# A graph network's batch-norm stage: the matrix engine's order within a tick, three turned buffers, merged row statistics, and eight tiles kept in SBUF

## The reference

```
x = _layernorm(x + _L2_gnn_ref(x, ...))       # third layer
x = _layernorm(x + _L3_gnn_ref(x, ...))       # fourth layer

# third layer, its end: batch norm over all rows, column by column
mean = jnp.mean(agg, axis=0); var = jnp.var(agg, axis=0)
y = (agg - mean) * jax.lax.rsqrt(var + BN_EPS) * gamma + beta
return jax.nn.relu(y)
# fourth layer, its start
h = (x @ W).reshape(n, heads, ch)             # 256 x 256, and the attention logits
```

## Time and profile before

| what | value |
|---|---|
| median of 3 runs | 6393.06 us (6388.5 to 6402.69) |
| the profiled execution's own time | 6399.0 us |
| its span, first to last instruction | 6397.3 us |
| mean granted TensorE clock over the span | 0.838 of full speed |
| phase n4 in the span, between the barriers | 4319.75 to about 4966.6 us |
| ticks 11 to 101 of n4 | 4367.76 to 4921.69 us |

### The profile page before, as it was taken

How to read it: one execution, slowest core, us unless ns; L and a number is a source line. 1 busy time by engine, 2 the same in 40 slices (tenths; PEclk the granted TensorE clock), 3 DMA queues, 4 the chain that set the end, 5 groups by cost and what they waited for, 6 DMA issues and landing times. The chain is left out here.

```text
span 6397.3 us, 74087 instructions
## 1 busy us (share of the span) xinstructions
PE 4260.0 (67%) x18797; PEld 3091.6 (48%) x18797; DVE 4604.8 (72%) x15011; ACT 3125.1 (49%) x6788; POOL 3809.3 (60%) x3139
## 2 busy tenths in 40 slices
PE   2488882058885988588866678997898477880000
PEld 1177772047774877477512224556777355560000
DVE  5645554644444876699599996968887899957776
ACT  0033331023332665588555556766776377772333
POOL 5767775767774777565255525721111688747776
PEclk9599996579997999799877778998999688895555
DMA  8944446954443997899698888989997678756665
GB/s 315 371 78 79 79 74 193 378 159 80 80 80 78 321 311 280 270 316 316 213 305 295 304 266 327 399 306 324 341 347 287 225 278 292 274 199 233 237 239 196
DMA packets 616389, 1558.26 MB, mean 244 GB/s; under 512 B 126988, under 2 KB 283090, under 8 KB 599038
## 3 DMA queue, kind: packets, MB, share of 16 engines
q1 hardware_dynamic: 430270, 1159.75, 51.8%
q0 software_dynamic: 185696, 393.77, 22.3%
HBM read 794.19 MB, written 811.66 MB: 251 GB/s over the span
## 5 line engine op out<-in xcount | busy, mean ns | idle before, releaser
L864 POOL DMA_INDIRECT NS<-e_tot,e_idx x392 | 633.5, 1616 | 241.5 <-ACT e_tot L1118 92.5
L1802 POOL DMA_INDIRECT l_eg<-HBT,k_nsrc x392 | 481.4, 1228 | 351.9 <-POOLq L161 120.6
L989 DVE TENSOR_SCALAR e_eq<-e_pk,z_skey 128x128 f32<-128x128 f32 x588 | 186.9, 345 | 627.6 <-DMA NS<-e_tot,e_idx 598.1
L2408 PE MATMUL l_pm<-k_w_L3b,l_zt 128*128 128x258 f32 x1568 | 414.2, 424 | 118.5 <-ACT l_o L2467 117.8
L1255 POOL DMA_INDIRECT XH<-n_o,z_home x392 | 384.2, 980 | 165.6 <-issue 113.1
L2382 PE MATMUL l_ps<-l_a,k_ident 128*128 128x512 f32 x392 | 309.0, 881 | 222.9 <-DVE l_a L2660 211.6
L2546 ACT ACTIVATE l_a<-l_a,l_eshare 128x64 f32<-128x64 f32 (+1 forms) x980 | 280.5, 373 | 308.8 <-DVE l_eshare L2064 308.8
L2408 PE MATMUL l_pm<-k_w_L1b,l_zt 128*128 128x264 f32 x1568 | 384.0, 400 | 51.1 <-ACT l_o L2467 50.8
L2022 DVE SCALAR_TENSOR_TENSOR l_erun<-l_erun,k_same,l_eg 128x260 f32<-128x260 f32 (+2 forms) x880 | 414.9, 471 | 3.3 <-issue 0.2
L2408 PEld LDWEIGHTS l_pm<-k_w_L3b,l_zt 128*128 128x128 f32 x1568 | 328.5, 215 | 180.6 <-issue 126.9
L2737 DVE BATCH_NORM_STATS2 l_bs<-l_a 128x6 f32<-128x256 f32 x1016 | 402.1, 413 | 1.3
(11 more groups left out here) (442 smaller groups left out, 13304.1 us busy)
## 6 DMA issues: line engine op xcount, KB each, us to landing
HBT<-l_o SPq DMA_DIRECT2D x196, 528.0 KB, 4.3
l_a<-HBT SPq DMA_DIRECT2D x156, 528.0 KB, 6.0
GSUMS<-l_erun SPq DMA_DIRECT2D x72, 1056.0 KB, 5.9
NS<-z_zero SPq DMA_DIRECT2D x100, 520.0 KB, 9.1
l_a<-XH SPq DMA_DIRECT2D x98, 528.0 KB, 6.0
HA<-n_o SPq DMA_DIRECT2D x98, 528.0 KB, 4.6
l_a<-HA SPq DMA_DIRECT2D x98, 528.0 KB, 6.8
X<-l_z SPq DMA_DIRECT2D x98, 520.0 KB, 7.7
```

The lines of the kernel that those rows point to most:

```text
L864: pool.indirect_dma_start(out=nodes, out_offset=bass.IndirectOffsetOnAxis(ap=idx[q % DEEP][:, k:k + 1], axis=0), in_=tot[q % 2][:, k, :], ...
L1802: pool.indirect_dma_start(out=self.g[b % self.ng][:, k, :], out_offset=None, in_=self.table, in_offset=bass.IndirectOffsetOnAxis(ap=self.i ...
L2408: last = pe.matmul(self.pm[h][:, i, 0:self.wc], zt[:, k, h * (J // 2) + i, :], self.weight[:, k, 0:self.wc], start=k == 0, stop=k == KC - 1)
```

## The change

The change has five parts.

- On PE the order within a tick becomes PROD, TURN, BACK. The lags of all stages stay as they are.
- The buffer `zt` exists three times (RT = 3) and no longer twice, and ACT's wait for it is relaxed to fit.
- `variance` no longer issues eight `bn_aggr` for a pair of tiles but three small operations on all eight rows at once (difference of the two half means, sums, square) and a last one that joins them. The adding of EPS moves from DVE to POOL, as an operation of its own ahead of the power. `shifts` halves the sum of means.
- The last eight tiles before the final one of l3 (KEPT) stay in SBUF: their X2 rows and their sums. l3 doesn't store their sums to AGG, and n4 takes these tiles first (`order`) and doesn't load them. The sums' buffers (RY) become eight and no longer four.
- The loads' waits and the places of the logits follow the new order of tiles.

The diff, cut:

```diff
--- before.py
+++ after.py
 MOVED = 40
+KEPT = [(1, t) for t in range(TR - LATE, TR)]
+KEEP_ROWS = len(KEPT) + 1
...
     LD, YR, BACK, ADD, VAR, NORM, TURN, ZT, PROD, EVICT, STORE = 0, 2, 3, 4, 5, 7, 8, 9, 10, 11, 12
-    RA, RY, RZ, RO = 9, 4, 4, 3
+    RT = 3
+    RA, RY, RZ, RO = KEEP_ROWS, len(KEPT), 4, 3
+    order = KEPT + [(r, t) for r in range(2) for t in range(TR) if (r, t) not in KEPT]
...
-                    if t is not None:
+                    if t is not None and t >= len(KEPT):
+                        n = order[t][0] * TR + order[t][1]
                         if t >= RA:
                             sp.wait_ge(s_z, t - RA + 1)
-                        if t >= RY:
-                            sp.wait_ge(s_y, t - RY + 1)
+                        sp.wait_ge(s_y, t - RY + 1)
                         sp.dma_start(a[t % RA][:], rows(T["X2"], t)).then_inc(s_in[t % RA], 16)
-                        sp.dma_start(y[t % RY][:], agg[:, :, t * BLK:(t + 1) * BLK]).then_inc(s_yin[t % RY], 16)
+                        sp.dma_start(y[t % RY][:], agg[:, :, n * BLK:(n + 1) * BLK]).then_inc(s_yin[t % RY], 16)
...
+                        pool.tensor_scalar(ve[b][:], ve[b][:], EPS, None, ALU.add).then_inc(s_eps, 1)
+                        pool.wait_ge(s_eps, q + 1)
                         pool.tensor_tensor(rs[b][:], ve[b][:], S["minus_half"][:, 0:w], ALU.pow).then_inc(s_rs, 1)
...
                 for tick in range(ticks):
-                    t = tile(tick, BACK)
+                    t = tile(tick, PROD)
                     if t is not None:
-                        pe.wait_ge(s_y, t + 1)
-                        if t >= 1:
-                            pe.wait_ge(s_u, t)
-                        for j in range(J):
-                            for k in range(KC):
-                                last = pe.transpose(py[:, j, k, :], yr[t % 2][:, k, j, :], S["ident"][:])
-                        last.then_inc(s_back, 1)
+                        pe.wait_ge(s_zt, t + 1)
+                        for h in range(2):
+                            if t >= 1:
+                                pe.wait_ge(s_o, 2 * t - 1 + h)
+                            for i in range(J // 2):
+                                for k in range(KC):
+                                    last = pe.matmul(pm[h][:, i, 0:RW], zt[t % RT][:, k, h * (J // 2) + i, :], weight[:, k, :],
+                                                     start=k == 0, stop=k == KC - 1)
+                            last.then_inc(s_m, 1)
                     t = tile(tick, TURN)
                     if t is not None:
                         pe.wait_ge(s_z, t + 1)
...
                             for j in range(J):
                                 last = pe.transpose(pt[:, k, j, :], z[t % RZ][:, j, k * P:(k + 1) * P], S["ident"][:])
                         last.then_inc(s_t, 1)
-                    t = tile(tick, PROD)
+                    t = tile(tick, BACK)
                     if t is not None:
-                        pe.wait_ge(s_zt, t + 1)
-                        for h in range(2):
-                            if t >= 1:
-                                pe.wait_ge(s_o, 2 * t - 1 + h)
-                            for i in range(J // 2):
-                                for k in range(KC):
-                                    last = pe.matmul(pm[h][:, i, 0:RW], zt[t % 2][:, k, h * (J // 2) + i, :], weight[:, k, :],
-                                                     start=k == 0, stop=k == KC - 1)
-                            last.then_inc(s_m, 1)
+                        pe.wait_ge(s_y, t + 1)
+                        if t >= 1:
+                            pe.wait_ge(s_u, t)
+                        for j in range(J):
+                            for k in range(KC):
+                                last = pe.transpose(py[:, j, k, :], yr[t % 2][:, k, j, :], S["ident"][:])
+                        last.then_inc(s_back, 1)
 
...
-                            act.wait_ge(s_m, 2 * (t - 1))
-                        act.activation(zt[t % 2][:], pt[:], ACT.Copy).then_inc(s_zt, 1)
+                        if t >= RT:
+                            act.wait_ge(s_m, 2 * (t - RT + 1))
+                        act.activation(zt[t % RT][:], pt[:], ACT.Copy).then_inc(s_zt, 1)
                     t = tile(tick, NORM)
...
-                        if t < TR:
-                            dve.tensor_copy(S["asd"][:, J * t + j0:J * t + j0 + J // 2, :], pm[h][:, :, D:RW])
+                        if not order[t][0]:
+                            col = J * order[t][1] + j0
...
-                    for j in range(w):
-                        var_lk.link(dve.bn_aggr(mv[b][:, j, :], bs[b][:, j, :]))
-                        if j % 2:
-                            yield
+                    if q >= 2:
+                        dve.wait_ge(s_nb, q - 1)
+                    var_lk.link(dve.tensor_tensor(gap[b][:], bs[b][:, :, 1], bs[b][:, :, 4], ALU.subtract))
+                    yield
+                    var_lk.link(dve.tensor_tensor(mv[b][:], bs[b][:, :, 1:3], bs[b][:, :, 4:6], ALU.add))
+                    yield
+                    var_lk.settle(dve)
+                    var_lk.link(dve.scalar_tensor_tensor(gap[b][:], gap[b][:], 0.25, gap[b][:], ALU.mult, ALU.mult))
+                    yield
                     var_lk.settle(dve)
                     if q >= 2:
                         dve.wait_ge(s_rs, q - 1)
-                    dve.tensor_scalar(ve[b][:], mv[b][:, :, 1], EPS, None, ALU.add).then_inc(s_var, 1)
+                    dve.scalar_tensor_tensor(ve[b][:], mv[b][:, :, 1], 1.0 / D, gap[b][:], ALU.mult, ALU.add).then_inc(s_var, 1)
...
-                    dve.scalar_tensor_tensor(nb[b][:], mv[b][:, :, 0], -1.0, rs[b][:], ALU.mult, ALU.mult).then_inc(s_nb, 1)
+                    dve.scalar_tensor_tensor(nb[b][:], mv[b][:, :, 0], -0.5, rs[b][:], ALU.mult, ALU.mult).then_inc(s_nb, 1)
...
+    def rows_of(self, u):
+        k = self.kept_at.get(self.tiles[u])
+        return self.a[u % self.ra] if k is None else self.kept[0][k]
+
+    def out_of(self, u):
+        k = self.kept_at.get(self.tiles[u])
+        return self.o[u % self.ro] if k is None else self.kept[1][k]
+
...
+        if now and self.kind != "l3b" and now[1:] not in self.kept_at:
             u, region, t = now
...
-            layer_phase(nc, S, "l3", dict(kind="gcn", rows=T["X2"], rw=SW, weight=S["w_L2"], out=T["AGG"], slots=FIRST),
+            kept = ([y.sb(f"rows{b}", [P, J, SW]) for b in range(KEEP_ROWS)], [y.sb(f"sums{b}", [P, KC, J * P]) for b in range(len(KEPT))])
+            layer_phase(nc, S, "l3", dict(kind="gcn", rows=T["X2"], rw=SW, weight=S["w_L2"], out=T["AGG"], slots=FIRST, kept=kept),
                         dict(table=T["X2"], tw=SW, index=S["nsrc32"], acc=T["SUMS"][0:PC, :]), first=12)
-            batch_norm_phase(nc, S, T)
+            batch_norm_phase(nc, S, T, kept)
```

More of the change, by code:

```diff
@@ L1387, in _, with batch_norm_phase @@
                     take_turns(parts)
-def batch_norm_phase(nc, S, T):
+def batch_norm_phase(nc, S, T, kept):
     tag = "n4"
@@ L1394, in batch_norm_phase @@
     LD, YR, BACK, ADD, VAR, NORM, TURN, ZT, PROD, EVICT, STORE = 0, 2, 3, 4, 5, 7, 8, 9, 10, 11, 12
-    RA, RY, RZ, RO = 9, 4, 4, 3
+    RT = 3
+    RA, RY, RZ, RO = KEEP_ROWS, len(KEPT), 4, 3
+    order = KEPT + [(r, t) for r in range(2) for t in range(TR) if (r, t) not in KEPT]
     with Scope(nc, tag) as s:
-        a = [s.sb(f"a{b}", [P, J, SW]) for b in range(RA)]
-        y = [s.sb(f"y{b}", [P, KC, J * P]) for b in range(RY)]
+        a, y = kept
         yr = [s.sb(f"yr{b}", [P, KC, J, P]) for b in range(2)]
@@ L1404, in batch_norm_phase @@
         mv = [s.sb(f"mv{b}", [P, 2 * J, 2]) for b in range(2)]
+        gap = [s.sb(f"gap{b}", [P, 2 * J]) for b in range(2)]
         ve = [s.sb(f"ve{b}", [P, 2 * J]) for b in range(2)]
@@ L1407, in batch_norm_phase @@
         nb = [s.sb(f"nb{b}", [P, 2 * J]) for b in range(2)]
-        zt = [s.sb(f"zt{b}", [P, KC, J, P]) for b in range(2)]
+        zt = [s.sb(f"zt{b}", [P, KC, J, P]) for b in range(RT)]
         py = s.ps("py", [P, J, KC, P])
@@ L1430, in batch_norm_phase @@
         s_frs = s.sem("batch_rstd")
+        s_eps = s.sem("variance_guarded")
         s_bn = s.sem("batch_factors")
@@ L1459, in pair @@
             return (t // 2, J * 2) if 0 <= t < TN and t % 2 else None
-        rows = lambda table, t: tile_rows(table, t // TR, t % TR)
+        rows = lambda table, t: tile_rows(table, *order[t])
         ticks = TN + STORE + 1
@@ L1556, in _ @@
                         act.wait_ge(s_t, t + 1)
-                        if t >= 2:
-                            act.wait_ge(s_m, 2 * (t - 1))
-                        act.activation(zt[t % 2][:], pt[:], ACT.Copy).then_inc(s_zt, 1)
+                        if t >= RT:
+                            act.wait_ge(s_m, 2 * (t - RT + 1))
+                        act.activation(zt[t % RT][:], pt[:], ACT.Copy).then_inc(s_zt, 1)
```

(32 more changed lines are left out.)

## The result

The changed kernel takes 6777.1 us (median of 4 runs, 6769.1 to 6784.9) against 6391.2 (4 runs, 6388.5 to 6402.7) before. The ratio is 1.060, 95% interval 1.0581 to 1.0619: 386 us slower. The forecast was 6815, with a range of 6630 to 6890.

The account below looks back on a forecast made before the run. The prediction took DVE, with POOL's round trip, to set the pace, and a closed chain plus clock loss to replace it: 423.5 - 3 - 1 + 3 = +422 us on 6393.1 makes 6815 us, range 6630 to 6890.

Parts of the forecast that it names:

- What bounded the kernel: Ticks 11 to 101 of n4: DVE sets the pace, POOL's round trip in its path, 6.15 us a tick.
- The closed chain: n4's ticks: eviction, PROD, TURN, BACK, add, eviction close once per tick, 8.96 us at full clock, +252.5 us over 90.
- The hole: PE idle in every tick of n4 from the end of BACK to PROD, 3.33 us.
- The clock: PE's products behind each hole slow down, 1.9 us a tick, making 10.86 us a tick and +423.5 us over 90.
- band of ticks: The main forecast's tick in n4, 10.2 to 11.9 us, chance 0.76, with its own range of 6750 to 6890 us.
- Three turned buffers: ACT's copy into `zt`: worth nothing in the steady ticks; after tick 101 -4 us, or -2 with a slower clock.
- Merged statistics: DVE and POOL in n4: worth 0 in the new chain, between -0.5 and +0.4 us a pair on the old path.
- Kept tiles, tick 10: 24 transfers spared, -1 us at l3's end; the first product group ahead of BACK in tick 10, +3 us.
- The clock holds: Rival for n4: the hole costs no clock, the tick is 8.96 us and the time 6644 us; chance 0.10.
- Losses pile up: Rival for n4: bursts run mostly at 1.2 GHz, tick 12 to 14 us, 6964 us at 12.5; chance 0.06.
- Not slower: Rival for n4: PROD needn't wait for its own tick's eviction, DVE keeps the pace, about 6387 us; chance 0.08.

Follow-up runs that it names:

- e5: The changed kernel, PE's new order kept, with DVE's whole eviction put ahead of shifts and the add: 6321.2 us, ratio 0.9881.
- e8: The changed kernel with PE's old order (BACK, TURN, PROD) and DVE's shifts moved behind the add: 6320.1 us, ratio 0.9887.
- e1: The changed kernel with PE's order alone put back to BACK, TURN, PROD: 6380.8 us, ratio 0.9973.
- e3: The changed kernel with 22 transpositions of the identity on PE ahead of each PROD, filling its hole: 6641.4 us, ratio 1.0389.
- e4: The changed kernel, PE's new order kept, with DVE's whole eviction put behind shifts but ahead of the add: 6392.4 us, ratio 0.9995.
- e7: The kernel before with the merged statistics and POOL's addition of EPS alone: 6388.3 us, ratio 0.9987.
- e2: The kernel before with PE's order alone changed to PROD, TURN, BACK: 6792.1 us, ratio 1.0614.
- e6: e5 with PE's old order, BACK, TURN, PROD: 6587.2 us, ratio 1.0294.

## Why the prediction was right

**What bounded the kernel.** It named DVE's path with POOL's round trip in it. e5 and e8 confirm that on the chip: beside e1 they take no work from any engine, only let DVE work on during the trip, and the stretch falls from 542 to 483 and 491 us.

**The closed chain.** Right in every link. The pieces were taken as 3.06, 0.15, 3.64, 0.93, 1.06 and 0.12 us, and the timeline after has 3.14, 0.15, 5.32, 0.88, 1.04 and 0.10. At full clock it was taken as 8.96 a tick, and e3 has 8.86. The hole was taken as 3.33 us and is 3.2 to 3.4 in 89 of the 90 ticks (4.80 in the first). That the chain closes over the DVE's add ahead of the eviction was only argued from the code; e4 shows it.

**The clock.** The mechanism was right, and this is the term that was mis-sized: 1.9 us a tick were taken, and 10.48 - 8.86 = 1.62 came. Over 90 ticks that is 25 of the 34 us by which +423.5 missed +389.5; the other 9 are the 0.1 us of the chain. The 1.9 was a mix of losses of 1.76 and 2.52 us with some ticks spared. In fact no tick was spared, but 83 of the 90 lost only 1.4 to 1.7 us against 3.80, one lost 2.1 and six lost 3.0. The mixture was wrong, and that its mean was near is in part luck. The forecast's band of ticks was also wider than its range of times: 11.9 us a tick would make 6909 us, past the 6890 that was named for it.

**Three turned buffers.** Nothing in the steady ticks, as forecast (e1 against e7). The tail was taken as 34.3 us and is 36.5 where it was 38.35: two of its groups still wait 0.60 us for an eviction, and the first comes with the slow clock. That is -2 where the sum has -3. With PE's old order the same buffer is worth more, -5.7 us (e1).

**Merged statistics.** Forecast at 0 in the new chain, and between -0.5 and +0.4 us a pair on the old path. In the new chain the shift still waits 1.77 us for POOL and DVE's next wait, for BACK, absorbs it. On the old path it measures -0.26 a pair (e7). The addition on POOL takes 0.24 us; the wait for POOL is 1.77 where it was 1.75, so what DVE saved is the gain.

**Kept tiles, tick 10.** Taken as -1 and +3. From the start of n4 to the add of tick 11 it is 47.0 us where it was 48.0; neither is big enough to be told from the spread of the phases around. The +3 for tick 10 didn't come: over the same stretch the changed kernel and e1, which differ in PE's order alone, both have 47.0 us, and e2 has 48.8 against the 48.0 of the kernel before.

**The rivals.** *The clock holds* gave 6644 and would have been right with a busy PE: e3 is 6641. It fell because no hole was spared. *Losses pile up* fell too; the worst group is 6.84 us, in six ticks of 90. *Not slower* needed a PROD that needn't wait for DVE's add; by the Trainium skill's page "Perfetto Trace Analysis", section "Optimizing Tensor Performance", rotating products through PSUM banks hides the eviction. The rule and the trace part here: with two halves of `pm` in both kernels it held where the eviction was free to run (wholly in e5, but for 71 us of waits in e4) and not where its instruction was queued behind a wait for the same engine's later work. The Trainium skill's advice on the same page, section "Identifying Performance Opportunities", is to improve the most-contended engine. Busy time alone wouldn't have named DVE here: PE is busy for 0.90 of the stretch of the earlier trace rows, DVE for 0.86, and the DMA share is 0.95; only the waits of the earlier trace rows name it. In the same 90 ticks, taking 0.26 us a pair from DVE's work gave 12 us (e7), and taking its wait away gave 51 (e8) and 59 (e5) more.

## What to carry to other kernels

Before two stages are swapped in one engine's program, write down each cross-engine wait together with what is queued ahead of it on both sides, and look for a ring that closes within one tick; its length, not any engine's busy share, is then the tick. Where an engine waits at the head of its tick for a helper's result, put work ahead that needs nothing of it: here moving one small operation was worth 1.0% (e8 against e1), while the larger rewrite cost 6%. And price a new hole on the matrix engine twice, once for what it adds to the chain and once for the clock behind it: 243 and 146 us in the 90 ticks here.

## What the runs showed of the hardware

- **The clock after short holes.** In the changed kernel all 89 holes of 3.2 to 3.4 us were followed by a slow group: 5.2 to 5.5 us in place of 3.8, and 6.84 in six of them, though the hole ahead of the long ones (3.39 us) is no longer than 18 others. The earlier trace rows have one after 2.88 us with no loss. In e6, of the two holes shown, 2.10 and 2.18 us, the one is followed by BACK and TURN in 2.56 us and products in 4.61, the other by 1.78 and 3.73: 1.66 us lost and none, at a mean granted clock of 0.91; 40 of e6's 90 groups of products were slow. So the length of the hole alone doesn't tell the loss; what else does stays open.
- **Idle work pays.** 22 transpositions of a constant in each hole brought the clock from 0.82 to 1.00 and the time down by 136 us (e3), though they were no part of the result.
- **The DMA share was no limit.** The earlier trace rows have 0.95 at 339 GB/s. e5 moved 387 GB/s in the same phase, at a share of 1.00 and with PE busy throughout. A share that near to 1 didn't keep the 90 ticks from becoming 13% shorter.
